# A transformer layer on eight cores: the query rope in five VectorE operations, and a normalisation in rows of 2048

## What is computed

```python
def layernorm(x, eps=1e-5):
    return (x - mean(x)) / sqrt(var(x) + eps)

def attn(x):                               # causal, 4 query heads share a k/v head
    q, k, v = x @ wq, x @ wk, x @ wv
    q = rms_norm(rope(q)); k = rms_norm(rope(k))
    return softmax(mask(q @ k.T / sqrt(128))) @ v @ wo

def rope(x):
    x1, x2 = split(x, 2)                   # 64 and 64 of a head's 128
    return concat([x1 * cos + x2 * sin, -x1 * sin + x2 * cos])

x = x + attn(layernorm(x))
x = x + (silu(h @ w_gate.T) * (h @ w_up.T)) @ w_down.T   # h = layernorm(x)
```

## Time and profile before

| | us |
|---|---|
| two timed runs | 6790.59 and 7036.0, median 6913.3 |
| the profiled execution | 6596.15 |
| its span (slowest of 8 cores; fastest 6548.3) | 6594.6 |
| TensorE busy | 5253.1 (80%) |
| ScalarE busy | 1357.2 (21%) |
| VectorE busy | 997.0 (15%) |
| phase 2, the slots | 916 to 3718 |
| phases 3 and 4 | 3772 to 6594 |

### The profile page before, as it was taken

One profiled execution on the slowest core, in us unless ns is written; L12 is line 12 of the kernel. 1 busy time (PEld: TensorE's weight loads), 2 busy tenths in 40 slices (PEclk: granted clock), 3 DMA queues, 4 the chain that ended last, 5 costly groups with the idle time before them and its releaser, 6 DMA issues. The chain is left out here.

```text
span 6594.6 us, 56545 instructions; the slowest of 8 cores (6548.3 to 6594.6 us)
## 1 busy us (share of the span) xinstructions
PE 5253.1 (80%) x20949; PEld 2026.4 (31%) x21360; DVE 997.0 (15%) x1236; ACT 1357.2 (21%) x1451; POOL 310.0 (5%) x382
## 2 busy tenths in 40 slices
PE   5777767656874788568886399999999997998998
PEld 1222222112221222122222144444444443443443
DVE  1222223114112400042000100000000000000000
ACT  1222213312531266115662000000000000000000
POOL 0000000000000000000000011111111110000000
PEclk8777778767876798778887699999999999999999
DMA  7445411122012200210002466666666666667764
GB/s 107 67 75 88 65 39 43 27 86 67 1 37 77 67 1 1 88 52 28 1 1 72 113 93 95 95 95 94 93 94 95 96 96 157 234 228 228 236 228 171
DMA packets 580666, 599.35 MB, mean 91 GB/s; under 512 B 342833, under 2 KB 453426, under 8 KB 580402
## 3 DMA queue, kind: packets, MB, share of 16 engines
q0 software_dynamic: 346016, 272.65, 27.2%
q1 hardware_dynamic: 234386, 323.06, 14.9%
HBM read 625.02 MB, written 125.83 MB: 114 GB/s over the span
## 5 line engine op out<-in xcount | busy, mean ns | idle before, releaser
L1279 PE MATMUL pDa<-gld,wdl 128*128 128x512 bf16 x4014 | 898.9, 384 | 139.4 <-DVE ost L1293 102.6
L1156 PE MATMUL pG<-ln2T,wgb 128*128 128x512 bf16 x4015 | 891.4, 379 | 83.4 <-DMA wub<-wuT 79.2
L1169 PE MATMUL pU<-ln2T,wub 128*128 128x512 bf16 x4013 | 889.6, 379 | 4.4
L886 ACT ACTIVATE probs<-pS,kbb,rsc 128x1024 bf16<-128x1024 f32 (+3 forms) x640 | 729.2, 1139 | 502.8 <-PE pS L859 317.9
L1279 PEld LDWEIGHTS pDa<-gld,wdl 128*128 128x128 bf16 x4096 | 404.5, 99 | 633.9 <-issue 163.0
L1156 PEld LDWEIGHTS pG<-ln2T,wgb 128*128 128x128 bf16 x4096 | 401.7, 98 | 564.2 <-issue 82.8
L1169 PEld LDWEIGHTS pU<-ln2T,wub 128*128 128x128 bf16 x4096 | 400.2, 98 | 483.9
L999 PE MATMUL pY<-lyT,wqb 128*128 128x512 bf16 x1001 | 296.3, 464 | 295.4 <-DMA wqb<-scr_wo 293.3
L1178 ACT ACTIVATE silo<-pG 128x2048 f32<-128x2048 f32 x64 | 120.1, 1877 | 1621.0 <-PE pG L1156 1621.0
L900 PE MATMUL pR<-probs,selb 128*1 128x512 bf16 (+3 forms) x1280 | 381.4, 381 | 90.5 <-ACT probs L886 47.4
L1181 DVE TENSOR_TENSOR gst<-silo,pU 128x2048 bf16<-128x2048 f32 x64 | 146.4, 2288 | 1680.4 <-PE pU L1169 1680.4
(11 more groups left out here) (115 smaller groups left out, 2566.6 us busy)
## 6 DMA issues: line engine op xcount, KB each, us to landing
gld<-scr_gated SPq DMA_DIRECT2D x64, 1024.0 KB, 6.6
wdl<-scr_wd SPq DMA_DIRECT2D x64, 1024.0 KB, 12.6
wdl<-scr_wd POOLq DMA_DIRECT2D x64, 1024.0 KB, 11.3
wgb<-wgT POOLq DMA_DIRECT2D x64, 512.0 KB, 12.3
wub<-wuT POOLq DMA_DIRECT2D x64, 512.0 KB, 19.2
wds<-wdT POOLq DMA_DIRECT2D x64, 512.0 KB, 20.6
scr_wd<-wds SPq DMA_DIRECT2D x64, 512.0 KB, 13.9
scr_gated<-gst SPq DMA_DIRECT2D x64, 512.0 KB, 13.1
```

Source lines behind the costliest of these rows:

```text
L886: rcol=rcol: e.activation(A(probs[g2], noff, [[1024, 128], [512, 2], [1, 512 - noff]]), A(pS[g2], noff, [[1024, 128], [512, 2], [1, 512 - ...
L1156: ctx.op("tensor", lambda e, dk=dk, gi=gi, buf=buf: e.matmul(pG[:, gi * 512:(gi + 1) * 512], wgb[buf][:, dk * 128:(dk + 1) * 128], ln2T[:, ...
L1169: ctx.op("tensor", lambda e, dk=dk, gi=gi, buf=buf: e.matmul(pU[:, gi * 512:(gi + 1) * 512], wub[buf][:, dk * 128:(dk + 1) * 128], ln2T[:, ...
L1279: pD=pD: e.matmul(pD[:, dki * 512:(dki + 1) * 512], wdl[buf][:, hci * DSW + dki * 128: hci * DSW + dki * 128 + 128], gld[buf][:, hci * 512 ...
```

## The change

It does two things. In `q_R` the two cosine multiplies become one of 128 partitions: x1 and x2 are the two halves of the same PSUM tile, and the cosine table is laid out twice on the host, so that csq has 128 partitions (its load, L709 before, too). Five operations are left. In `emit_norm` four blocks of 512 are done by one operation: 4 multiplies and 4 subtractions of 2048 columns, whose PSUM operand has a step of 0 in its outer dimension and so is read four times over. The intermediate goes to xr4v, since lnt2 has 512 columns only.

```diff
-        m["cosq"] = np.ascontiguousarray(cosT[perm_q].T)
+        cq = cosT[perm_q].T
+        m["cosq"] = np.ascontiguousarray(np.concatenate([cq, cq], axis=0))
...
-            csq = asb("csq", [64, 512])
+            csq = asb("csq", [128, 512])
...
-                        out=csq[:, :], in_=A(dram["cosq"].tensor, slot * 512, [[OWN, 64], [1, 512]])),
+                        out=csq[:, :], in_=A(dram["cosq"].tensor, slot * 512, [[OWN, 128], [1, 512]])),
...
-                        ctx.op("vector", lambda e, x1=x1, ro=ro: e.tensor_mul(ro[0:64, :], x1, csq[:, :]),
+                        ctx.op("vector", lambda e, qp=qp, ro=ro: e.tensor_mul(ro[:, :], qp, csq[:, :]),
                                waits=[("tm", mq["proj"][qc]), ("d_cs", m_cs)])
                         ctx.op("vector", lambda e, x2=x2: e.tensor_mul(tmpq[0:64, :], x2, snq[:, :]))
                         ctx.op("vector", lambda e, ro=ro: e.tensor_add(ro[0:64, :], ro[0:64, :], tmpq[0:64, :]))
-                        ctx.op("vector", lambda e, x2=x2, ro=ro: e.tensor_mul(ro[64:128, :], x2, csq[:, :]))
                         ctx.op("vector", lambda e, x1=x1: e.tensor_mul(tmpq[64:128, :], x1, snq[:, :]))
...
-                        for hb in range(DK):
-                            ctx.op("vector", lambda e, hb=hb, xbq=xbq: e.tensor_tensor(
-                                lnt2[:, :], xbq[:, hb * 512:(hb + 1) * 512],
-                                pR[:, 0:512], ALU.mult),
+                        NB4 = min(4, DK)
+                        for hb in range(DK // NB4):
+                            ctx.op("vector", lambda e, hb=hb, xbq=xbq, NB4=NB4: e.tensor_tensor(
+                                A(xr4v, 0, [[NH * 256, 128], [512, NB4], [1, 512]]),
+                                A(xbq, hb * NB4 * 512, [[DK * 512, 128], [512, NB4], [1, 512]]),
+                                A(pR, 0, [[1024, 128], [0, NB4], [1, 512]]), ALU.mult),
                                 waits=([("tm", m_bc3), ("d_l20", ctx.c("d_l20"))] if hb == 0 else []))
-                            ctx.op("vector", lambda e, hb=hb: e.tensor_tensor(
-                                A(ln1q, hb * 512, [[DK * 512, 128], [1, 512]]),
-                                lnt2[:, :], pR[:, 512:1024], ALU.subtract),
+                            ctx.op("vector", lambda e, hb=hb, NB4=NB4: e.tensor_tensor(
+                                A(ln1q, hb * NB4 * 512, [[DK * 512, 128], [512, NB4], [1, 512]]),
+                                A(xr4v, 0, [[NH * 256, 128], [512, NB4], [1, 512]]),
+                                A(pR, 512, [[1024, 128], [0, NB4], [1, 512]]), ALU.subtract),
                                 waits=([("tm", m_bc4)] if hb == 0 else []))
```

More of the change, by code:

```diff
@@ L203, in build_program @@
         ("wgT", [D, DH], F32), ("wuT", [D, DH], F32), ("wdT", [DH, D], F32),
-        ("cosq", [64, OWN], F32), ("sinq", [64, OWN], F32),
+        ("cosq", [128, OWN], F32), ("sinq", [64, OWN], F32),
         ("cosk", [64, KEXT], F32), ("sink", [64, KEXT], F32),
```

## The result

The changed kernel takes 0.9937 of the time before, with a 95% interval of 0.9914 to 0.996. Its undisturbed executions lie between 6546.0 and 6568.5 us (eight, mean 6559); those of the kernel before, taken beside them, at 6597.5 and 6603.6. A second measurement on another occasion gave 0.9931 (0.9898 to 0.9964). That is 41 to 47 us: faster, since neither interval reaches 1, and by less than 2%. Many executions of either kernel are disturbed, with a lower clock on one or both dies, and take 6700 to 7300 us; the ratios leave them out, and the two times shown of before (6790.6 and 7036.0) were both such.

What follows compares the result with a forecast made beforehand. In Q stages no engine was full: the later of the rope's chain and the projection's set each round, and the normalisation was bare. Rope 18.0 plus normalisation 25.6, said as 43, off the 6913.3 median gave 6870 us; range 6553 to 6993.

Steps and rivals of the forecast that it cites:

- the normalisation's part: Normalisation behind each slot: 8 wide operations for 32, 6.2 us less at slots 1 to 3, 7.0 after slot 3; 25.6.
- the rope's 18: Q-stage rounds: one cosine multiply goes, rope 0.78 us shorter, 18 us saved in all; bounds 0 and 50.
- Sum: Whole kernel: 18.0 + 25.6 = 43.6, said as 43 us, subtracted from the median of 6913.3, giving 6870.
- The chance of "same": Whole kernel: 0.84 for a change not told from none; about 2%, 138 us, taken as what a measurement can tell.
- 59 in all: Normalisation's upper bound: gain if a 2048-column operation ran at twice the rate of the rows, costing 1.2 us.
- The rule on tiles of at least 512 elements: Normalisation: read as a threshold, the old width was enough, this term near 0 and the total gain 18 us.
- The cosine table's load, 0: Table load in each slot, doubled to 128 partitions: 6.2 us still hidden, so 0; without cover up to 3 a slot.
- In the 40 rounds that TensorE ended this gives 0: Q-stage rounds where the projection ended last, 40 of 64: the shorter rope saves nothing there.
- 24 x 0.75: Q-stage rounds where VectorE ended last, 24 of 64: each gains its lateness of 0.75 us, 18 us in all.
- Rising and falling clock: TensorE's clock in the rounds: rising, all projections early, 6791 us, chance 0.14; falling, all rounds 10.07 us, 6961, chance 0.08.
- less idle time should not lower a clock: Argument against the rival where Q-stage rounds fall to TensorE's low clock, 6961 us, chance 0.08.
- The rule that TensorE starts a group at the low clock: Q-stage projections: cited as favouring the rival where shorter idle stretches keep the clock up, 6791 us, chance 0.14.

Runs made afterwards that it cites:

- The small matmuls' run: Changed kernel with slot 0's 16 small matmuls ahead of each projection in slots 1 to 3 too, result unused: one time, 6516.2 us, no interval.

## Why the prediction was right in its size and wrong in its level

- **The size.** 43 us less on the profiled execution's own 6596.2 is 0.9935. Measured were 0.9937 and 0.9931. The match is better than its working: the normalisation's part came as worked out, the rope's 18 came as some 17 by two errors that nearly cancel (below), which is luck, and some 6 us of the 44 were lost ahead of the feed-forward in code that is the same.
- **The level.** The step that failed is in "Sum": "I subtract the same 43 from the median: 6870 us". The median of before stood on the executions of 6790.6 and 7036.0 us; the profiled one, at 6596, stands at the level that the changed kernel's times are compared with, and its 6553 was the number to give. The changed kernel's median was 6567, and eight of its thirteen times lie from 6546 to 6569. The sentence that nothing in the change depends on what separates the executions was true, but it gives no reason to choose the median's level. For the same fault the range was wide at the top (up to 6993), and its low end, 6553, cut through the measured group, since it left no room below the one profiled execution.
- **The chance of "same".** The change is below 2%, as forecast. That the scatter could be read as 2% either way was wrong: the compared executions of the changed kernel lie within 0.4% of each other in the first measurement and 1% in the second, and 0.6% is clear of noise.
- **The normalisation, 25.6 us.** Right: 6.2 at slot 1 and 7.0 at the end, in the rows. (The bound "59 in all" for twice the rate is 60 when the last slot is counted with its 26.1 us, as the term itself does.) The rule on tiles of at least 512 elements ("VectorE: DVE Perf Modes", on the TRN2 errata, in the Trainium skill), read as a threshold, is refuted by the trace: 32 operations of 512 columns took 25.3 us, 8 of 2048 took 19.1.
- **The cosine table's load, 0.** Right: no rope waited for it, and its landing took 2.8 us at most.
- **The rope, 18 us.** The sum was near (14.0 in the rounds and 0.8 for each slot's first rope, some 17), but the step "In the 40 rounds that TensorE ended this gives 0", with "24 x 0.75" for the others, failed. It took the rounds that the projection ends as fixed. (Its 24 also holds the first square of each slot, which ends no round; of the 60 rounds on that core VectorE ended 20.) In slot 0 the projection's rounds were not fixed: before, 7.5 of 15 a core ended with the projection, at a mean of 8.75 us; now 14 do, at 7.64, with a granted clock of 0.94 instead of 0.89. Rounds of 8.9 us came with every second round before and with every fourth or fifth after, and so 11.7 us came instead of the six that its seven late rounds held. In slots 1 to 3 the late rounds got shorter (a median of 8.16 to 7.37 us), but fewer are late (14.8 to 10.8 of 45 a core), long rounds grew from 11.9 to 15.4, the clock fell from 0.80 to 0.77, and 2.3 us came instead of 12.
- **The rivals.** Rising and falling clock were put as all or nothing. Both happened at once, one in slot 0 and the other in slots 1 to 3. The argument "less idle time should not lower a clock" failed in slots 1 to 3, where the long rounds became more. The small matmuls' run shows what does raise it there: 1.05 us of work in TensorE's idle stretch ahead of each projection brought the clock from 0.77 to 0.91 in the mean of the cores and took 43 us away. The rule that TensorE starts a group at the low clock when it idled between groups ("TensorE: Matmul & The Clock Gate", on the oscillation, in the Trainium skill) agrees in its direction. As a rule for the single projection it isn't borne out, since 0.83 us of idle time stand ahead of the one of 6.51 us and of the one of 4.94.
- **Open.** What exactly decides at which round the clock falls, and so why the shorter rope lowered it in slots 1 to 3. It is not the program alone, since two cores with the same start in the same execution differ by 6.5 us.

## What to carry to other kernels

When a round waits for the later of two chains, work out what the other chain does once it is the only one left: here TensorE's chain ran at 1.2 or 2.4 GHz depending on how it was kept busy, and a cut on VectorE paid only where TensorE had small work in its waits. Joining short VectorE operations is safe money where nothing covers them: count 0.26 us for each operation that goes, since the 1.04 ns a column stay (f32, from 512 to 2048 columns). And before a time is forecast, ask which of a kernel's times the profile stands for: here a median of two lay 4.8% above the profiled execution, seven times the size of the change.

## What the runs showed of the hardware that was not expected

- 768 more matmuls (16 for each of 48 heads) made the kernel about 48 us faster: they kept the clock of three Q stages at 0.90 instead of 0.72 to 0.76 (core 3; the 48 us are the difference of two mean spans).
- In one execution, two cores with the same program and the same start (1468.4 us) took 127.9 and 134.4 us for the same 15 rounds.
- Rounds in which no instruction was changed changed their length with the start of the stage: by 9 us over three slots behind a shorter normalisation with the old rope, and by 8.5 us with its width at 1024 instead of 2048.
